# Value products of the merged stage: one 128-column stationary operand against two of 64 columns

## The chip, the cores and the metric

The kernel runs on one core of a Trainium2 chip. The metric is the device time of one execution in microseconds (us). TensorE (PE) multiplies, VectorE (DVE) and ScalarE (ACT) work element by element, GpSimd (POOL) does masks, powers and indirect transfers, SyncE (SP) issues most DMAs.

## The reference, cut to what matters

A block of 8 sequences of 512 tokens, width 1024, fp32. First an mLSTM attention with 16 heads of 64, gated and added to x; then a layernorm and a mixture of 16 experts (two per token) with a shared feed-forward network, gated and added.

```
C  = qk * D                               # per head: 512 x 512, lower triangle, decayed
Cn = C / (normalizer + EPS)
h  = einsum('bhst,bhtd->bhsd', Cn, vh)    # the value products
x  = x + tanh(g_xattn) * (layernorm of h per head, times ln_scale)
x  = x + tanh(g_ffn) * (shared(xn) + routed(xn))      # xn = layernorm(x)
```

## The kernel before, in words

The program is two blocks, one after the other.

**The merged stage** (`mix_block`) handles the 4096 tokens in 32 chunks of 128. The chunk has number c = 4b + j: b is the sequence, j its chunk of four. Attention runs chunk by chunk: within a chunk the products of 128 queries with 128 keys, and a `state` (per head 64 x 65) that carries what came before in the sequence, so for j = 0 there is no state to read and for j = 3 none to write. The same stage computes layernorm, router and the first half of the shared feed-forward network (`gate_up`, L1009, and `stage_y`, L1022) for earlier chunks. `ORDER` is a list written out by hand: each of 35 turns goes through the items of `TURN`, each for its own chunk (offset), and every engine does its part of each item in that order. So every engine runs its own fixed queue, and semaphores are the only coupling.

In a turn TensorE comes, in this order, to these items. A2 is the gate products (L978). B0 and B1 are the scores (L1033), H1 a transpose (L946), A3 the gate rows (L984). **B2** is the value products of heads 0 to 7, and with j > 0 their state products (L1051). Then come Y1 to Y4 (L1022), with B1 and A5 between them; A5 transposes the gate rows (L991) and waits for the semaphore `rows_rdy`, which VectorE raises with L723. N1 transposes the first half of xn into `p_tr` (L946). **B3** is the value products of heads 8 to 15. A6 is a tiny product for the decay (L996). N2 transposes the second half of xn into the same `p_tr`, so it waits until ScalarE (L555) and VectorE (L863) have read the first half. After that come G1 to G6 (L1009), B4 (L1078: the new state, j < 3), E3 (L1090, router, waits for L863 on the second half), Q2, Q3, and K7, K8 (L1009).

The value products of a group of four heads are the loop at L1044 and L1045. The stationary operand is `cmat` of a head (128 keys in the partitions, 128 query tokens as columns), the moving operand `ctx_v` (128 keys, 64 values and a column of ones, so 65 columns). The result, 128 tokens x 65, goes into the bank `p_u[g % 2]`. `start` is set for the first head of a group, `stop` only where no state product follows. All operands are fp32, and in the trace each such product is two MATMUL records and two LDWEIGHTS records: 8 heads are "x16".

The state products of B4 (L1078) have the same moving operand, and 64 stationary columns (`ks`, one head); the even heads write partitions 0 to 63 of the bank, the odd ones 64 to 127.

VectorE makes `cmat` (L752, two groups for B2, two for B3), which raises `c_rdy`. ScalarE copies the results out (L595) when `u_ps` is raised.

**The VectorE chain that ends at L723.** After gate-up of the turn is done: ScalarE's tanh (L617), VectorE L869, L872, then L800 (needs the power of GpSimd, L469, which needs L792), L694, L752 twice, L878, L698, L699, L808 (needs GpSimd L477, which stands behind L469 and two indirect DMAs, L490), L810 to L814, L704 to L723. L792 comes earlier in the turn, behind L737, which needs ScalarE's L547, which needs the transfer of the row `mid_s_row` (SP, L364).

**The expert stage** (`ffn_block`) is 105 tiles of 128 rows; the change doesn't touch it.

Of the kernel before, what the change touches and what calls it, by code (L numbers as in the profile page):

```python
# [11 lines left out]
P = 128  # L12
# [7 lines left out]
HV = DH + 1  # L20
# [14 lines left out]
def ge(eng, sem, n):  # L35

    if isinstance(n, int) and n <= 0:
        return
    eng.wait_ge(sem, n)
# [32 lines left out]
def mix_block(nc, t, keep):  # L72
# [3 lines left out]
    with ExitStack() as ctx:  # L76
        def sb(name, shape, dt=f32):
            return ctx.enter_context(nc.sbuf_tensor(name, shape, dt))

        def pb(name, shape, dt=f32):  # L80
            return ctx.enter_context(nc.psum_tensor(name, shape, dt))
# [27 lines left out]
        cmat = stage[:, 8, :].rearrange("p (n g s) -> p n g s", n=2, g=HG)  # L109
        x = stage[:, 10, :]  # L110
        sq = stage[:, 11, :].rearrange("p (h d) -> p h d", h=NH)
        ctx_v = sb("ctx_v", [P, 2, NH, HV])
# [14 lines left out]
        rows = sb("rows", [NH, 4, P])  # L127
# [17 lines left out]
        p_u = [pb(f"p_u{n}", [P, 512]) for n in range(2)]  # L145
# [92 lines left out]
        def heads(g):  # L238

            return [8 * (g // 2) + g % 2 + 2 * n for n in range(HG)]  # L240
# [694 lines left out]
        def _(pe):  # L935
# [101 lines left out]
            def values(b, j, gs):  # L1037
                c = b * CPB + j
                for g in gs:
                    pe.wait_ge(c_rdy, NG * c + g + 1)  # L1040
                    ge(pe, u_rdy, NG * c + g - 1)
                    if g < 2:
                        ge(pe, state_rdy, 2 * states_done(b, j))
                    for n, h in enumerate(heads(g)):  # L1044
                        last = nc.tensor.matmul(p_u[g % 2][:, n * HV:(n + 1) * HV], cmat[:, g % 2, n, :], ctx_v[:, j % 2, h, :],  # L1045
                                                start=(n == 0), stop=(j == 0), skip_group_check=True)
                if j > 0:
                    for n, pair in enumerate(zip(heads(gs[0]), heads(gs[1]))):
                        for h in pair:
                            lo = DH * (h % 2)  # L1050
                            last = nc.tensor.matmul(p_u[h % 2][:, n * HV:(n + 1) * HV], qs_t[lo:lo + DH, j % 2, h // 2, :],  # L1051
                                                    state[lo:lo + DH, h // 2, :], start=False, stop=True,
                                                    skip_group_check=True)
                last.then_inc(u_ps, 2)

            def states_done(b, j):
                return (CPB - 1) * b + j

            def stage_b(part, b, j):
                c = b * CPB + j  # L1060
                if part < 2:
                    scores(b, j, (2 * part, 2 * part + 1))
                if part == 2:
                    if j > 0:
                        pe.wait_ge(qs_sb, scaled_before(b, j) + 1)
                    pe.wait_ge(cv_in[j % 2], 16 * (2 * b + j // 2) + 16)
                    values(b, j, (0, 1))
                if part == 3:
                    values(b, j, (2, 3))
                if part == 4:  # L1070
                    if j < CPB - 1:
                        pe.wait_ge(ks_rdy, states_done(b, j) + 1)
                        for m in range(2):
                            pe.wait_ge(u_rdy, NG * c + 3 + m)
                            for n in range(8):
                                h = 8 * m + n
                                lo = DH * (h % 2)
                                last = nc.tensor.matmul(p_u[m][lo:lo + DH, (n // 2) * HV:(n // 2 + 1) * HV],  # L1078
                                                        ks[:, h, :], ctx_v[:, j % 2, h, :], start=True, stop=True)
                            last.then_inc(ds_ps, 1)  # L1080
# [557 lines left out]
```

## Time and profile before

| | |
|---|---|
| time, median of 3 runs | 3005.92 us (3003.09 to 3010.25) |
| the profiled execution's own time | 2988.08 us |
| its span | 2986.5 us |
| TensorE busy | 2848.8 us (95%) |
| VectorE busy | 1869.6 us (63%) |
| mean granted TensorE clock | 0.986 of full speed |

The span is that of the profiled execution; 1.6 us of its time lie outside. The merged stage takes roughly the first 1120 us, the experts the rest. A busy TensorE is a row of matmul records whose ends are modelled and overlap, so that its pace is to be read from starts.

### The profile page before, as it was taken

The numbers are of one execution on the slowest core, as the hardware profiler recorded it, in microseconds if no ns is written. First come the engines' busy times: TensorE is split into PE (matmuls) and PEld (weight loads), VectorE is DVE, ScalarE is ACT, GpSimd is POOL, SyncE is SP. The second block draws the span as 40 slices with busy tenths as digits, with TensorE's granted clock in tenths as the row PEclk, the third lists the DMA queues.
The fourth block names the chain that finished last, engine by engine and source line by source line (L and its number), as shares of the span: only waits on it lengthen the run. The fifth ranks groups of instructions, "written<-read, shape, count | busy, mean of one in ns | idle before, by whom it ended". The sixth has DMA issues, their size and how long they took to land.

```text
span 2986.5 us, 47577 instructions
## 1 busy us (share of the span) xinstructions
PE 2848.8 (95%) x16422; PEld 2354.5 (79%) x16423; DVE 1869.6 (63%) x3213; ACT 1008.7 (34%) x1916; POOL 978.6 (33%) x1089
## 2 busy tenths in 40 slices
PE   4799999999999997999999999999999999999999
PEld 3688888888888875788888888888888888888887
DVE  3788888888888865454554545545545446565665
ACT  4444444444444421233333333333333331111111
POOL 1333333334333423443343343433434411111111
PEclk9799999999999998999999999999999999999999
DMA  6445445554555442344444344443444325444544
GB/s 194 143 152 173 143 150 152 165 157 151 150 164 154 149 149 81 138 148 148 142 148 145 141 155 141 147 148 142 148 146 144 116 98 162 158 158 149 167 141 161
DMA packets 229289, 441.87 MB, mean 148 GB/s; under 512 B 98832, under 2 KB 115088, under 8 KB 228624
## 3 DMA queue, kind: packets, MB, share of 16 engines
q1 hardware_dynamic: 123504, 333.62, 32.6%
q0 software_dynamic: 35008, 73.10, 7.8%
q10 hardware_dynamic: 70656, 33.56, 4.4%
q8 instruction: 73, 1.20, 0.2%
q14 instruction: 48, 0.39, 0.0%
HBM read 350.83 MB, written 107.18 MB: 153 GB/s over the span
## 4 chain that ended last, share of the span: by engine, by line
PE 57%; DVE 1%; ACT 1%; issue 0%; ACTq 0%; DMA 0%; POOL 0%; POOLq 0%; DVEq 0%
PE p_g_b L1561 19%; PE p_up_b L1561 19%; PE p_y_b L1549 18%; PE p_h_b L1536 2%; DVE w_lo L1411 1%; ACT w_hi L1353 1%; ACTq L1194 0%; DMA xn<-mid_xn,idx_q 0%; DVE x_t_b L1437 0%; ACTq L1179 0%; DMA idx<-mid_lists 0%; POOL idx L1289 0%; POOL xn L1299 0%; DVE x L1477 0%; DVE x L1468 0%
## 5 line engine op out<-in xcount | busy, mean ns | idle before, releaser
L1299 POOL DMA_INDIRECT xn<-mid_xn,idx_q x288 | 306.0, 1063 | 565.0 <-DVE x_t_b L1437 474.7
L1561 PE MATMUL p_g_b<-w_hi,xt_hi_b 128*128 128x512 f32 x840 | 339.6, 404 | 29.5 <-DVE w_lo L1411 13.4
L1427 DVE TENSOR_TENSOR ht_lo_b<-p_h_b,ht_hi_b 128x512 fp32r<-128x512 f32 x105 | 72.3, 689 | 470.8 <-ACT ht_hi_b L1365 470.8
L1549 PE MATMUL p_y_b<-w_hi,ht_hi_b 128*128 128x512 f32 x840 | 327.1, 389 | 1.9 <-DVE ht_lo_b L1427 1.9
L1561 PE MATMUL p_up_b<-w_hi,xt_lo_b 128*128 128x512 f32 x840 | 328.6, 391 | 0.0
L1561 PE MATMUL p_g_b<-w_hi,xt_lo_b 128*128 128x512 f32 x840 | 328.5, 391 | 0.0
L1561 PE MATMUL p_up_b<-w_hi,xt_hi_b 128*128 128x512 f32 x840 | 328.5, 391 | 0.0
L1561 PE MATMUL p_up_b<-w_lo,xt_hi_b 128*128 128x512 f32 x840 | 328.4, 391 | 0.0
L1561 PE MATMUL p_g_b<-w_lo,xt_hi_b 128*128 128x512 f32 x840 | 327.9, 390 | 0.0
L1549 PE MATMUL p_y_b<-w_hi,ht_lo_b 128*128 128x512 f32 x840 | 326.9, 389 | 0.0
L1549 PE MATMUL p_y_b<-w_lo,ht_hi_b 128*128 128x512 f32 x840 | 326.9, 389 | 0.0
L1411 DVE TENSOR_TENSOR w_lo<-stage,w_hi 128x1024 fp32r<-128x1024 f32 x200 | 230.0, 1217 | 80.0 <-ACT w_hi L1360 52.6
L1437 DVE STREAM_TRANSPOSE x_t_b<-xn 128x1024 f32<-128x1024 f32 x105 | 237.0, 2257 | 21.5 <-DMA xn<-mid_xn,idx_q 10.2
L1365 ACT ACTIVATE ht_hi_b<-p_h_b 128x512 fp32r<-128x512 f32 x105 | 62.9, 599 | 546.5 <-PE p_h_b L1536 546.5
L1396 ACT ACTIVATE th_b<-p_g_b 128x512 f32<-128x512 f32 x105 | 62.8, 598 | 520.5 <-PE p_up_b L1561 520.5
L1449 DVE SCALAR_TENSOR_TENSOR th_b<-th_b,p_g_b 128x512 f32<-128x512 f32 x105 | 72.1, 687 | 254.7 <-ACT th_b L1396 254.7
L1009 PE MATMUL p_g<-w_hi,xt 128*128 128x512 f32 x512 | 212.4, 415 | 0.0
L1561 PEld LDWEIGHTS p_g_b<-w_hi,xt_hi_b 128*128 128x128 f32 x840 | 158.5, 189 | 65.5 <-DVE w_lo L1411 19.0
L1009 PE MATMUL p_up<-w_hi,xt 128*128 128x512 f32 x512 | 201.7, 394 | 0.0
L1549 PEld LDWEIGHTS p_y_b<-w_hi,ht_hi_b 128*128 128x128 f32 x840 | 157.7, 188 | 34.9 <-DVE ht_lo_b L1427 2.2
L1561 PEld LDWEIGHTS p_up_b<-w_lo,xt_hi_b 128*128 128x128 f32 x840 | 158.2, 188 | 33.9
L1561 PEld LDWEIGHTS p_g_b<-w_hi,xt_lo_b 128*128 128x128 f32 x840 | 158.2, 188 | 33.9
(223 smaller groups left out, 5797.0 us busy)
## 6 DMA issues: line engine op xcount, KB each, us to landing
mid_y<-y_b SPq DMA_DIRECT2D x73, 512.0 KB, 2.6
stage<-mid_g_row SPq DMA_DIRECT2D x64, 512.0 KB, 5.6
stage<-in_eg SPq DMA_DIRECT2D x16, 2048.0 KB, 8.9
stage<-in_eu SPq DMA_DIRECT2D x16, 2048.0 KB, 15.2
stage<-in_ed SPq DMA_DIRECT2D x16, 2048.0 KB, 19.4
mid_y<-in_x SPq DMA_DIRECT2D x34, 512.0 KB
stage<-in_x SPq DMA_DIRECT2D x32, 512.0 KB
stage<-in_ctx_t ACTq DMA_DIRECT2D x32, 512.0 KB, 8.5
```

What stands on the lines that cost most here:

```text
L1009: last = nc.tensor.matmul(out[:, :], xt[:, a, k, :], w[:, k, o:o + FE], start=(k == 0 and m == 0), stop=(k == KD - 1 and m == 2))
L1299: nc.gpsimd.indirect_dma_start(out=xg_parts[:, n, :], out_offset=None, in_=xn_flat, in_offset=bass.IndirectOffsetOnAxis(ap=idx_q[:, n:n + ...
L1353: nc.scalar.activation(w_hi[:, p, :], stage[:, p, :], ACT.Copy).then_inc(gu_hi, 1)
L1365: nc.scalar.activation(ht_hi[:, :, :], p_h[:, :, :], ACT.Copy).then_inc(ht_hi_rdy, 1)
L1396: nc.scalar.activation(th[:, :], p_g[:, :], ACT.Tanh, scale=0.5).then_inc(tanh_rdy, 1)
L1411: nc.vector.tensor_tensor(w_lo[:, p, :], stage[:, p, :], w_hi[:, p, :].bitcast(f32), ALU.subtract).then_inc(sem_lo, 1)
L1427: nc.vector.tensor_tensor(ht_lo[:, :, :], p_h[:, :, :], ht_hi[:, :, :].bitcast(f32), ALU.subtract).then_inc(ht_rdy, 1)
L1437: nc.vector.transpose(x_t[:, :, :].rearrange("p k (j t) -> p t k j", t=4), xg_parts[:, :, :].rearrange("p t (i k) -> p t k i", k=KD)).then ...
L1449: nc.vector.scalar_tensor_tensor(out=th[:, :], in0=th[:, :], scalar=1.0, in1=p_g[:, :], op0=ALU.add, op1=ALU.mult).then_inc(silu_step, 1)
L1536: last = nc.tensor.transpose(p_h[:, k, :], h[:, k * P:(k + 1) * P], ident[:, :])
L1549: last = nc.tensor.matmul(p_y[n][:, :], a[:, k, :], b[:, GUP + k, w], start=(k == 0 and m == 0), stop=(k == FE // P - 1 and m == 2))
L1561: mm = nc.tensor.matmul(out[:, :], a[:, k, :], w[:, k, o:o + FE], start=(k == 0 and m == 0), stop=(k == KD - 1 and m == 2))
```

## The change

Each value product is written as two. The first takes columns 0 to 63 of `cmat` of the head (tokens 0 to 63) and writes partitions 0 to 63 of `p_u`, the second takes columns 64 to 127 and writes partitions 64 to 127. Both have the same moving operand. `start` and `stop` are as before, for either half. The number of products at this line goes from 512 to 1024.

```diff
                     for n, h in enumerate(heads(g)):
-                        last = nc.tensor.matmul(p_u[g % 2][:, n * HV:(n + 1) * HV], cmat[:, g % 2, n, :], ctx_v[:, j % 2, h, :],
-                                                start=(n == 0), stop=(j == 0), skip_group_check=True)
+                        for o in (0, P // 2):
+                            rows = slice(o, o + P // 2)
+                            last = nc.tensor.matmul(p_u[g % 2][rows, n * HV:(n + 1) * HV], cmat[:, g % 2, n, rows],
+                                                    ctx_v[:, j % 2, h, :], start=(n == 0), stop=(j == 0),
+                                                    skip_group_check=True)
```

## Rows read from the trace of the kernel before

**Rows 1.** The page: busy time of each engine, share of the span, instructions
```profile
PE 2848.8 (95%) x16422; PEld 2354.5 (79%) x16423; DVE 1869.6 (63%) x3213; ACT 1008.7 (34%) x1916; POOL 978.6 (33%) x1089
```

**Rows 2.** Stretches: length, busy PE, PEld, DVE, ACT, POOL, granted clock, DMA share, GB/s
```profile
75.00:150.00 75.00, 58.83 (x487) 50.81 (x486) 56.21 (x123) 35.40 (x76) 24.09 (x15) 0.73 0.48 142
...
450.00:600.00 150.00, 145.24 (x1174) 120.91 (x1174) 127.46 (x307) 68.13 (x166) 56.02 (x39) 1.00 0.52 160
```

**Rows 3.** Waits, 150 to 1050 us: waiter <- releaser: total us, times, longest
```profile
PE p_small L978 <- issue: 22.0, 27, 0.8
PE p_small L991 <- DVE rows L723: 2.7, 7, 0.6
...
ACT stage L547 <- DMA stage<-mid_s_row: 9.7, 10, 1.8
```

**Rows 4.** TensorE by time (start us, us): B2 of a chunk with j > 0
```profile
510.12 2.00 PE L1045 MATMUL p_u<-ctx_v,stage 128*128 128x65 f32 x16
512.04 1.11 PE L1051 MATMUL p_u<-state,stage 64*128 64x65 f32 x16
```

**Rows 5.** The same turn: N1, B3 and the state products behind it
```profile
520.44 0.60 PE L946 MATMUL p_tr<-ident,xn 128*128 128x128 f32 x4
520.87 1.90 PE L1045 MATMUL p_u<-ctx_v,stage 128*128 128x65 f32 x16
522.70 1.11 PE L1051 MATMUL p_u<-state,stage 64*128 64x65 f32 x16
```

**Rows 6.** The same turn: end of G1, B4 and start of E3
```profile
525.16 0.39 PE L1009 MATMUL p_g<-w_lo,xt 128*128 128x512 f32 x1
525.39 0.40 PE L1009 MATMUL p_up<-w_lo,xt 128*128 128x512 f32 x1
525.72 1.15 PE L1078 MATMUL p_u<-ctx_v,stage 128*64 128x65 f32 x32
526.80 1.96 PE L1090 MATMUL p_small<-rw,xt 128*128 128x32 f32 x16
```

**Rows 7.** Instructions on p_u: ns min/median/max, first and last start, form
```profile
L1045 PEld LDWEIGHTS p_u<-ctx_v,stage x1024: 186/192/338, 40.8 to 1091.0; 128*128 128x128 f32 x171
...
L1078 PEld LDWEIGHTS p_u<-ctx_v,stage x768: 132/138/232, 54.0 to 1059.7; 128*64 128x64 f32 x192
```

**Rows 8.** Two turns with j = 0: B2, and L723 with A5 behind it
```profile
309.74 2.00 PE L1045 MATMUL p_u<-ctx_v,stage 128*128 128x65 f32 x16
311.55 0.71 PE L1022 MATMUL p_g<-w_hi,ht 128*128 128x512 f32 x2
...
316.34 0.27 DVE L723 SCALAR_TENSOR_TENSOR rows<-fcum,gmax 16x128 f32<-16x128 f32 x1
...
317.17 0.35 PE L991 MATMUL p_small<-ident,rows 16*128 16x16 f32 x3
...
450.41 0.27 DVE L723 SCALAR_TENSOR_TENSOR rows<-fcum,gmax 16x128 f32<-16x128 f32 x1
...
450.83 0.33 PE L991 MATMUL p_small<-ident,rows 16*128 16x16 f32 x3 [0.37 <-DVE rows L723]
```

**Rows 9.** L723 and A5 in the turn of rows 4
```profile
517.32 0.27 DVE L723 SCALAR_TENSOR_TENSOR rows<-fcum,gmax 16x128 f32<-16x128 f32 x1
...
518.72 0.29 PE L991 MATMUL p_small<-ident,rows 16*128 16x16 f32 x2
```

**Rows 10.** A turn with j = 0: L863 on the first half, then N2
```profile
320.36 0.69 DVE L863 TENSOR_TENSOR xt<-p_tr,xt 128x512 fp32r<-128x512 f32 x1 [0.47 <-ACT xt L555]
...
321.54 0.66 PE L946 MATMUL p_tr<-ident,xn 128*128 128x128 f32 x4
```

**Rows 11.** ScalarE and VectorE later in the turn of rows 4
```profile
531.80 1.06 ACT L547 ACTIVATE stage<-stage 128x1024 f32<-128x1024 f32 x1 [0.38 <-DMA stage<-mid_s_row]
...
534.58 1.22 DVE L737 SCALAR_TENSOR_TENSOR stage<-stage 128x1024 f32<-128x1024 f32 x1
...
540.07 0.69 DVE L869 SCALAR_TENSOR_TENSOR th<-th,p_g 128x512 f32<-128x512 f32 x1 [1.63 <-ACT th L617]
```

## The prediction

> **What bounds the kernel now.** I read the page first for the busiest engine, then the stretches of the merged stage, then the waits, then TensorE in order of time around the changed line. On the page TensorE is busy 95% of the span, the next engine 63% [rows 1]. In the middle of the merged stage TensorE is busy 145.2 of 150 us at the full clock, but VectorE is close behind it with 127.5 [rows 2]. The list of waits tells how much TensorE stands still from 150 to 1050 us: 22.0 us ahead of L978, 0.8 in each of 27 turns, and 2.7 us at A5, where it waits for VectorE's L723 in 7 of the 27 [rows 3]. The rest is its own queue, back to back. So a microsecond taken from TensorE's queue is one off the stage, as long as VectorE, GpSimd and the transfers have results ready that much sooner. Before 150 us it is otherwise: TensorE is busy 58.8 of 75 us and has 0.73 of its clock [rows 2].
>
> **What a value block costs now.** Busy times overlap, so I go by starts. B2 takes 512.04 - 510.12 = 1.92 us with state products behind it [rows 4], and 311.55 - 309.74 = 1.81 with none [rows 8]. B3 takes 522.70 - 520.87 = 1.83 [rows 5]. For 16 passes (8 heads, two each) that is 0.114 to 0.120 us a pass. There are 64 such blocks (1024 passes) [rows 7].
>
> **What it will cost.** The new form, 128 rows by 64 stationary columns, 65 moving ones, fp32, halves of a bank in turn, is in the trace already: it is B4. Its 32 passes take 526.80 - 525.72 = 1.08 us, 0.034 a pass [rows 6], less than a third of a full-width one. Two things can explain it, and the change gets both: the weight load is shorter (138 against 192 ns) [rows 7], and two passes on different halves of the columns run side by side. A changed block is 8 heads x 2 halves x 2 passes = 32 passes, so 1.08 us. Two differences from B4 remain. Both halves stream the same moving operand, where in B4 they are two heads; I cost that at nothing, since neither half can need more than its own read. And the state products behind it are a third form (64 rows by 128 columns).
>
> For that exit: L1045 ahead of the state products took 0.11 us more than ahead of Y1 (1.92 against 1.81). L1078 ahead of L1090 is a change of form too, so some of it is in the 1.08. Bounds 1.08 and 1.20; I take 1.14. For the entry: L1078 starts 0.33 us after the L1009 before it, where two L1009 are 0.23 apart [rows 6], so entering the narrow form costs 0.10. B3 comes from full-width transposes and pays it anew; B2 comes from the 16-column products of A3 and changes form today, so I put nothing there (bounds 0 and 0.10).
>
> The Trainium skill (TensorEngine Tiling (Array Packing), Key Properties) says that changing the tiling mode drains TensorE. This trace agrees, with 0.10 us for one change. By the rule alone, with 0.10 at every entry and exit, a block would save 0.1 less than I reckon, some 6 us over 64 blocks.
>
> So B2 saves 1.92 - 1.14 = 0.78 us (0.62 to 0.84), B3 saves 1.83 - 1.14 - 0.10 = 0.59 (0.53 to 0.75).
>
> **What of it reaches the end of the turn.** TensorE arrives earlier at everything behind B2 and B3, and three results may not be there.
>
> A5 waits for L723. In the turn of rows 4, L723 ends at 517.59 and A5 starts at 518.72, 1.13 later [rows 9]. In a turn that waits the gap is 450.83 - 450.68 = 0.15 [rows 8], so that is its least and the slack here 0.98: B2's 0.78 goes through. The 7 turns that wait already [rows 3] give nothing. With j = 0 there are no state products between, and in the turn of rows 8 that doesn't wait the gap is 317.17 - 316.61 = 0.56, so 0.4 goes through. Taking A5 of each turn in the same way, of the 28 turns from 140 us to 1050 us 21 have j > 0, and 4 of them no slack, the other 17 at least 0.65; of the 7 with j = 0, 3 have none and 4 have 0.4. B2 then brings 17 x 0.78 + 4 x 0.4 = 14.9 us.
>
> N2 waits for L863, which runs from N1, ahead of B3, and not from B3. With j = 0, L863 ends at 321.05 and N2 starts at 321.54 [rows 10]; with a least gap like that of A5 some 0.34 goes through. With j > 0 the state products, 1.11 us [rows 5], stand there as well, and the whole 0.59 does. B3 brings 21 x 0.59 + 7 x 0.34 = 14.8 us.
>
> The third is a transfer. The scaled queries are reloaded by a DMA whose start hangs on L723, not on B2 or B3. ScalarE's L547 behind it ends at 532.86, and VectorE takes it up at 534.58 [rows 11]: 1.72 us of slack, and the turn gets up to 1.37 shorter. That holds, barely. But ScalarE waited for this transfer 10 times, up to 1.8 us [rows 3], and there VectorE will wait. VectorE has 1.63 us of idleness ahead of L869 [rows 11] that hides this from TensorE at the end of the turn; not hidden is L792, from which GpSimd's power, its list writes, L808 and so L723 of the next turn follow. I take 0.3 us for each of 10 such turns, 3 us (bounds 0 and 10 x 1.37).
>
> The four turns outside, the first three and the last, have 8 blocks. In the first ones TensorE waits for VectorE, and what it does sooner only makes it wait longer; the last is like the others. I take 2 us for all (bounds 0 and 8).
>
> Within B2 the second group of heads will be asked for sooner, half a new block after the start (about 0.55 us where it was 0.96). L752 makes it just ahead; I cost this at nothing, at most 0.1 a turn, 3 us. Nothing on SP or POOL is added or moved, and ScalarE copies the same tiles.
>
> **Sum.** 14.9 + 14.8 + 2 - 3 = 28.7, say 29 us. The profiled execution took 2988.1, so 2959. The median of the runs shown is 3005.9, 18 us above that execution, and what separates them isn't in the trace; the saving is the same, and I forecast 3005.9 - 29 = 2977 us. All low ends together (B2 17 x 0.62 + 1.6, B3 21 x 0.53 + 2.4, less 14 and 3) leave 9 us, all high ones (17 x 0.84 + 1.6, 21 x 0.75 + 2.4, and 8) 42.
>
> **Rivals.**
>
> *All of it arrives.* A slack that grows along with the change (VectorE too gets its inputs sooner) would let every block through: 64 x (0.78 + 0.59) / 2 = 44 us, 2962. Against it: the chain to L723 starts ahead of B2. 12%.
>
> *VectorE and the transfer take over.* VectorE is at 127.5 of 150 us [rows 2]; in turns 1.4 us shorter it is at 89%, in order and with waits inside. If the late reload delays L792 in most turns, A5 waits in all of them, B2's gain is gone and B3's is halved in the turns with j = 0 and one in three of the others: about 10 us, 2996. For it are the 7 waits at A5 and the 10 of L547; against it that A5's median slack is 0.98. 22%.
>
> *The halves don't run side by side.* This is the slow side. The new passes share rows and moving operand, only the columns differ. Two passes of B4 take 2 x 0.034 = 0.0675 us; if they alternate two heads' data and that is what lets them overlap, 32 passes in a row cost 32 x 0.0675 = 2.16 us, with the exit 2.22. A block gets 0.3 (B2) to 0.49 (B3, with entry) slower, 64 x 0.4 = 25 us, 3031. It decides from 1.83 / 32 = 0.057 us a pass on. Against it is that B4 has the same rows for both halves too, and 0.034. 5%.
>
> Beside it: the Trainium skill (TensorE: Matmul & The Clock Gate, Part 3, The mechanism) says that a weight load overlaps a running matmul only when the row group differs. The passes of one block all have all rows, so by that rule they would stand in line. In B4 they do too, and 0.034 us a pass is less than half of either of its instructions' times, so this trace speaks against the rule for halves of the columns.
>
> *No difference* through something not seen, within 6 us: 7%, and slower for other causes (the granted clock falls below 1.00 in the middle of the stage): 1%.
>
> **How the numbers follow.** The forecast's own case has 53%; since its ends are not likely to meet, it spans some 18 to 38 us, 2968 to 2988. A measurement of this kernel can tell 0.2%, 6 us, from no change. Faster takes the forecast, the first rival and most of the second: 87%. Same 7%, slower 6%. For 8 in 10 the range reaches from 2960, just past where all of it arrives, to 2994, most of the way to the second rival.
>
> **What would show each step.** In the changed profile L1045's successor (the same loop) has x32 in a block, and starts 1.1 to 1.2 us apart from what follows, at full clock; 1.8 or more and the side-by-side step is wrong. The wait of L991 for L723 grows from 2.7 us and 7 times to some 10 us and 15 to 20 times; if it is in nearly all turns with over 0.5 us each, the second rival is right. N2 begins to wait in the turns with j = 0 only. VectorE's L737 waits for L547 in about 10 turns, and its wait at L869 shrinks. From 1200 us on nothing changes but the start. If the turn, 33.3 us on average now (27 of them in 900 us) [rows 3], is not 0.8 to 1.3 shorter, the prediction is wrong.

## The result, and the profile after

| | before | after |
|---|---|---|
| median of the runs | 3006.78 us (4 runs, 3003.09 to 3010.25) | 2981.11 us (4 runs, 2978.03 to 2983.26) |
| the profiled execution's own time | 2988.08 us | 2982.64 us |
| its span | 2986.5 us | 2981.0 us |

The ratio is 0.9914, with a 95% interval of 0.9901 to 0.9926: 26 us faster (22 to 30), where I forecast 29 and 2977 us. The two profiled executions are only 5.4 us apart. The one of before is 19 us under its median, the one of after 1.5 us over its own, so the two traces can't simply be subtracted.

The page after, busy time of each engine, and the stretch in the middle of the merged stage (columns as in [rows 2]):
```profile
PE 2798.5 (94%) x17446; PEld 2296.2 (77%) x17447; DVE 1876.4 (63%) x3213; ACT 1009.0 (34%) x1916; POOL 981.1 (33%) x1089
```
```profile
450.00:600.00 150.00, 139.41 (x1320) 114.07 (x1319) 130.35 (x301) 68.98 (x166) 56.77 (x39) 1.00 0.53 159
```
TensorE has 50.3 us less busy time than in [rows 1], and in the middle of the stage 139.4 us of 150 instead of 145.2 [rows 2]. It now stands still in places where it did not before.

TensorE in order of time, B2 and B3 of a turn with j > 0. The changed loop is now L1047; what stands behind it in the program has moved by three lines (L1051 is L1054, L1078 is L1081, L1090 is L1093):
```profile
508.55 1.15 PE L1047 MATMUL p_u<-ctx_v,stage 128*64 128x65 f32 x32
509.63 1.11 PE L1054 MATMUL p_u<-state,stage 64*128 64x65 f32 x16
...
517.76 0.26 PE L991 MATMUL p_small<-ident,rows 16*128 16x16 f32 x2 [1.37 <-DVE rows L723]
...
519.45 0.60 PE L946 MATMUL p_tr<-ident,xn 128*128 128x128 f32 x4
519.98 1.15 PE L1047 MATMUL p_u<-ctx_v,stage 128*64 128x65 f32 x32
521.06 1.11 PE L1054 MATMUL p_u<-state,stage 64*128 64x65 f32 x16
```
Both blocks take 1.08 us from start to start, where they took 1.92 and 1.83 [rows 4, 5]. Ahead of A5 (L991) TensorE stands still for 1.37 us, which eats all that B2 saves in this turn.

From the list of waits, 150 to 1050 us (total us, times, longest):
```profile
PE p_small L991 <- DVE rows L723: 17.2, 15, 2.5
...
DVE gparts L694 <- remote: 15.2, 12, 1.5
...
PE p_small L984 <- DVE gparts L694: 11.9, 14, 1.1
...
DVE stage L737 <- ACT stage L547: 5.7, 5, 2.4
...
PE p_u L1047 <- issue: 4.4, 6, 1.4
PE p_small L996 <- DVE decm L730: 3.6, 6, 0.6
```
The wait at A5 has grown from 2.7 to 17.2 us [rows 3], more than the some 10 us expected. Three others of TensorE are new: L984 waits for VectorE's L694, L1047 has idle time ahead of it, and L996 (A6) waits for L730.

**What stands behind L984.** Another turn of the changed kernel, the engines by time:
```profile
236.12 1.08 PE L978 MATMUL p_small<-stage,w_gate 128*32 128x128 f32 x32 [0.81 <-issue]
...
236.50 1.06 POOL L490 DMA_INDIRECT mid_lists<-tok,posi  x1 [0.19 <-issue]
...
238.23 0.66 PE L946 MATMUL p_tr<-ident,th 128*128 128x128 f32 x4
...
239.59 0.35 DVE L694 TENSOR_SCALAR gparts<-p_small,gate_bias 128x128 f32<-128x128 f32 x1 [1.51 <-remote]
239.81 0.60 ACT L623 ACTIVATE ht<-p_tr 128x512 fp32r<-128x512 f32 x1 [3.78 <-PE p_tr L946]
...
240.00 0.61 PE L984 MATMUL p_small<-gparts,fold 128*16 128x128 f32 x4 [1.11 <-DVE gparts L694]
```
and a turn of the kernel before:
```profile
406.01 1.06 POOL L490 DMA_INDIRECT mid_lists<-tok,posi  x1 [0.18 <-issue]
...
406.73 1.08 PE L978 MATMUL p_small<-stage,w_gate 128*32 128x128 f32 x32 [0.81 <-issue]
...
408.61 0.34 DVE L694 TENSOR_SCALAR gparts<-p_small,gate_bias 128x128 f32<-128x128 f32 x1
...
409.42 0.61 PE L984 MATMUL p_small<-gparts,fold 128*16 128x128 f32 x4
409.53 0.60 ACT L623 ACTIVATE ht<-p_tr 128x512 fp32r<-128x512 f32 x1 [2.90 <-PE p_tr L946]
```
L694 reads the result of L978, whose matmuls end at 237.20. In the turn of before L694 starts 1.88 us after L978's start, here 3.47 after, and VectorE is idle meanwhile. ScalarE's L623 needs only the transposes that start at 238.23, and waits as well.

The trace also keeps the time of every semaphore signal. In the turn above L978's comes 2.64 us behind the start of its last matmul, and L694 starts 0.02 us behind the signal. So the signal itself is late, and VectorE takes it up at once. Below I call these late signals. From 130 us on there are 28 turns. In the first trace of before L978's signal comes 0.31 us behind that start in all of them, here over 0.8 us behind in 18, at most 2.66. What comes in the first 1.07 us costs nothing, since VectorE isn't free for L694 before.

Where they occur they go with the place of the list writes (GpSimd's two indirect DMAs, L490) in the turn. In this trace all 22 turns in which the first write starts between 1.03 us ahead of L978's last matmul and 0.17 us behind it have a signal 0.6 us or more behind; the 6 turns in which it starts 0.4 us or more behind that matmul have none, 0.31 us as in the kernel before. But the first trace of before has writes in those same places, and no late signal.

### The profile page after: what moved, and what is told of

Same layout as the page of the kernel before. It is cut to its first block, busy times and chain, and to the rows that moved or that the text cites. A ratio compares the mean times of both kernels' runs of the same rounds, so it can differ in the third digit from the quotient of the medians.

```text
span 2981.0 us, 49625 instructions
## 1 busy us (share of the span) xinstructions
PE 2798.5 (94%) x17446; PEld 2296.2 (77%) x17447; DVE 1876.4 (63%) x3213; ACT 1009.0 (34%) x1916; POOL 981.1 (33%) x1089
## 4 chain that ended last, share of the span: by engine, by line
PE 57%; DVE 1%; ACT 1%; issue 1%; ACTq 0%; DMA 0%; POOL 0%; POOLq 0%; DVEq 0%
PE p_g_b L1564 19%; PE p_up_b L1564 19%; PE p_y_b L1552 17%; PE p_h_b L1539 2%; DVE w_lo L1414 1%; ACT w_hi L1356 1%; ACTq L1197 0%; DMA xn<-mid_xn,idx_q 0%; ACT xt_hi_b L1374 0%; DVE x_t_b L1440 0%; ACTq L1182 0%; DMA idx<-mid_lists 0%; POOL idx L1292 0%; POOL xn L1302 0%; DVE x L1480 0%
## 5 line engine op out<-in xcount | busy, mean ns | idle before, releaser
L584 ACT ACTIVATE stage<-stage,cols 128x128 f32<-128x128 f32 x512 | 154.2, 388 | 96.4 <-POOL stage L454 96.4
```

Source lines behind the costliest of these rows:

```text
L584: nc.scalar.activation(gbd[:, h, :], gbd[:, h, :], ACT.Exp, bias=cols[:, j, 0, h:h + 1]).then_inc(d_rdy, 1)
```

## The experiments

Each was compared with runs of the kernel before on the same chip. The first four shared one chip (kernel before: 3005.3 us), the next four a second (3001.6), the last four a third (2990.4). The kernel before and the changed kernel, unedited, have traces on the first chip only (the chip of the result's two isn't on record).

**1 and 2: the two kernels again.** No edit.

> The kernel before, unchanged, for a second trace of it. The profiled execution of before took 2988 us, its four timed ones 3003 to 3010, and the changed kernel's trace shows something that before's doesn't: the semaphores that TensorE raises at L978, L1033 and L946 (A2, B0, H1) reach VectorE and ScalarE up to 2.7 us after the last matmul where 0.3 is usual. Theory D (density): the narrow passes cause it, so this trace has none of it, at any span. Theory E (execution): it comes and goes with the execution, costs the kernel before the 18 us that part 2988 from 3006, and this trace has a span near 3004 with waits of VectorE's L694 or L752 of about 15 to 20 us in the merged stage. Time against before: ratio 1.000 within 0.002 by both.

> The changed kernel, unchanged, on the same chip as the kernels beside it. By the working of the prediction 26 to 29 us less than before, ratio 0.990 to 0.992. Theory D: the late semaphores at A2 to H1 are there again in about 15 of 28 turns. Theory E: their number differs from the first trace, and the time goes with it.

Before: 3006.67 us (ratio 1.0004, 0.9993 to 1.0014); after: 2979.32 us (0.9914, 0.9899 to 0.9929). Waits of before, 150 to 1050 us, in an execution nearer to its median (3000.96 us):
```profile
DVE gparts L694 <- remote: 4.4, 4, 1.4
PE p_small L991 <- DVE rows L723: 4.2, 11, 0.6
PE p_small L984 <- DVE gparts L694: 3.3, 5, 1.0
PE p_u L1045 <- issue: 2.6, 2, 1.3
```
The kernel before has late signals too, and the trace I predicted from just had none. By their own times there are as many as in the changed kernel (18 of 28 turns over 0.8 us, 19 in the changed kernel's second trace). They cost it less: past the point where VectorE is free for L694 they reach 7.7 us in all, in the changed kernel's two traces 17.3 and 15.1 (150 to 1050 us). The waits of L694 and L752 that theory E put at 15 to 20 us are 6.9.

This execution also shows the granted clock at 0.5 (1.2 GHz) for 6.8 us (length, busy PE, PEld, DVE, ACT, POOL, granted clock, DMA share, GB/s):
```profile
742.00:750.00 8.00, 5.89 (x74) 4.65 (x72) 5.90 (x17) 1.71 (x3) 7.27 (x4) 1.00 0.44 157
750.00:756.80 6.80, 6.80 (x35) 5.53 (x33) 6.41 (x18) 2.57 (x5) 0.62 (x2) 0.51 0.20 46
```
TensorE had been busy 5.89 of the 8 us ahead of it. In the first trace of before the clock is 1.00 from 150 to 1050 us throughout. In the changed kernel's second trace L984 waits for L694 12 times, 8.9 us, and L991 for L723 13 times, 14.7 us.

**3 and 4: one half of the change alone.** `B2 only`: heads 0 to 7 split, heads 8 to 15 as before. `B3 only`: the other way.
```diff
-                        for o in (0, P // 2):
-                            rows = slice(o, o + P // 2)
+                        for o, m in (((0, P // 2), (P // 2, P // 2)) if g < 2 else ((0, P),)):
+                            rows = slice(o, o + m)
```

> Only B2 (groups 0 and 1) is split, B3 stays at full width. Theory 1 (the working of the prediction): each B2 0.78 us shorter, A5 absorbs some, 15 us less than before, ratio 0.995. Rival (VectorE's chain to L723 is the bound at A5 in most turns): B2's gain is gone there, 0 to 4 us, ratio 0.999 to 1.000, and TensorE's wait at L991 grows by about what B2 saved.

> Only B3 (groups 2 and 3) is split. Theory 1: 0.59 us in each turn with j > 0, 0.34 with j = 0: 15 us less than before, ratio 0.995, and the sum of this run's and the last one's gains is that of the whole change. Rival (VectorE and the reload bound the turn): the first of the two splits brings most and the second little, so that each alone gives 20 us or more.

B2 only: 2994.15 us, ratio 0.9966 (0.9953 to 0.9978), 10 us. B3 only: 2999.58 us, 0.9980 (0.9968 to 0.9992), 6 us. Both expectations are missed: each part was to give 15 us, and the parts give 16 together, the whole 26. Waits of B2 only, then of B3 only:
```profile
PE p_small L991 <- DVE rows L723: 23.7, 16, 2.5
...
PE p_small L984 <- DVE gparts L694: 4.7, 9, 0.7
```
```profile
PE p_small L984 <- DVE gparts L694: 11.1, 14, 1.0
...
PE p_u L1047 <- issue: 7.0, 11, 1.2
...
PE p_small L996 <- DVE decm L730: 4.1, 7, 0.6
```
Most of what B2 alone doesn't bring is lost at A5, and much of B3's at L984, L1047 and A6. The trace of B3 only is that of its slowest execution, 9 us over its median, with the granted clock at 0.5 for 20.4 us between 150 and 1050 us, so its waits are at the high end. Why the whole loses less at A5 (14.7 to 17.2 us) than B2 alone (23.7) isn't settled.

**5 and 6: no list writes.** Here a small power on GpSimd takes the place of each of the two list writes, in both kernels (1.35 us each, the writes 1.20). It leaves out what the writes do: the lists stay zero, so the experts gather other rows, as many as before.
```diff
-                        nc.gpsimd.indirect_dma_start(
...
+                        nc.gpsimd.tensor_tensor(idle[:, k, :], idle[:, k, :], mhalf[:, 0:5], ALU.pow).then_inc(done, 1)
```

> The kernel before, where GpSimd doesn't write the token lists: each of its two indirect DMAs a turn (L490) is an arithmetic instruction of about the same length, so that its queue keeps its timing. What is left out: the lists stay zero and the experts get token 0's rows; tiles and their number stay. Theory S (the late signals come with GpSimd's indirect DMAs beside A2, B0 and H1): no late signal at A2 in this trace, and the merged stage ends some 10 to 18 us sooner, as in the first trace of before. Theory N (they have nothing to do with them): late signals at A2 in over half the turns, as in the second trace of before, and the merged stage ends within 4 us of that.

> The same omission in the changed kernel. Theory S: no late signals, and the change is worth here what the prediction's working gives without them, 29 us less than the run beside it (within 5). Theory N: late signals in 20 of 28 turns as before, and the difference to the run beside it is the 26 us of the full kernels.

Before: 2978.76 us (0.9915, 0.9901 to 0.9929); after: 2945.43 us (0.9805, 0.9790 to 0.9819). Without list writes the change is worth 33.3 us, and no signal of L978 is late. Waits of TensorE from 150 to 1050 us without list writes, in the kernel before (these are all), then the larger ones in the changed kernel:
```profile
PE p_small L978 <- issue: 22.0, 27, 0.8
PE p_small L1090 <- DVE xt L863: 1.5, 7, 0.5
```
```profile
PE p_small L978 <- issue: 19.5, 24, 0.8
PE p_small L991 <- DVE rows L723: 6.8, 7, 1.4
PE p_small L996 <- DVE decm L730: 4.2, 7, 0.6
...
```
The kernel before gains 22.8 us by it, but not all of that is late signals: the undisturbed execution, with list writes and none late, took 2988. Up to the last L978 the two traces take the same time (1039.3 and 1040.0 us); the 5 us by which the trace without list writes is shorter lie behind it, where the experts gather other rows. In the changed kernel without list writes A5 starts at its least gap behind L723, 0.15 to 0.17 us, in 21 of 28 turns: here VectorE's chain is what TensorE runs up against next.

**7 and 8: list writes at the end of the turn** (an item of their own behind D1; on GpSimd they then run behind L477).

```diff
...
-                "E4", "W6", "Z1", "U1", "D1", "K7", "K8", "Q3")
+                "E4", "W6", "Z1", "U1", "D1", "M1", "K7", "K8", "Q3")
...
```

> The kernel before, all of its work, with GpSimd's two list writes of a turn moved behind L477 of the same turn, so that they start about 4.5 us after A2 instead of 0. GpSimd's L477 comes 0.8 us sooner at best. Theory S: the late signals leave A2, B0 and H1 and could turn up 4 us later, beside B2 and B1; time 5 to 15 us less than before. Theory N: late signals at A2 as ever; time within 3 us of before, or up to 5 less for the earlier L477.

> The changed kernel with the same move. Here A5 waits for L723, and L723 for L477, in half of the turns, so that the earlier L477 counts. Theory S: 10 to 20 us less than the changed kernel, 2960 to 2970. Theory N: 3 to 8 us less, 2972 to 2977.

Before: 2999.55 us (0.9996, 0.9985 to 1.0007); after: 2980.02 us (0.9916, 0.9901 to 0.9931). No signal of L978 is late in either, and the time has not moved. No theory holds whole: in the first S had 5 to 15 us less and N late signals as ever, in the second both had 2977 us or less. Other waits are there instead. Changed kernel with the writes moved (its lines behind L487 stand three further on: L697 is L694, L539 is L536, L981 is L978, L987 is L984):
```profile
POOL stage L454 <- DMA stage<-mid_g_row: 138.8, 51, 6.3
...
PE p_small L987 <- DVE gparts L697: 13.1, 19, 1.0
...
PE p_small L981 <- ACT stage L539: 12.2, 15, 0.8
```
GpSimd waits 138.8 us for the reload of the gating row, in the changed kernel 47.5. L987 waits for L697 as long as it did with late signals, so that wait alone doesn't tell of them.

The four kernels of this chip have no late signal at all, and none of them has the list writes in their old place. So experiments 5 to 8 by themselves don't tell whether the writes or the chip make the difference; for the writes speaks their place in the turns of the traces above.

**9: halves apart.** Loops over heads and halves exchanged; the same 32 passes, but eight in a row on the same columns.
```diff
-                    for n, h in enumerate(heads(g)):
-                        for o in (0, P // 2):
+                    for o in (0, P // 2):
+                        for n, h in enumerate(heads(g)):
```

> The changed kernel with the loops over heads and over halves exchanged: first all passes on columns 0 to 63 of four heads, then all on columns 64 to 127. The same 32 passes in a block, the same shapes, but 8 passes in a row (4 heads, two each) go to the same half of TensorE, and halves change once in a group of four heads. Theory A (the halves run side by side, and that is what makes a pass 0.034 us; alone, a pass of this shape takes over half of a full-width one, some 0.058 us): the block takes 32 x 0.058 = 1.9 us against 1.09 in the changed kernel, and the time is within -5 to +15 us of the kernel before. Rival B (the pass is short because its weight load is of 64 columns and not 128, in whatever order): a block takes 1.05 to 1.15 us and the time stays at the changed kernel's 2980 us, within 4. Between 1.2 and 1.7 us a block both have a share, and the block's start-to-start says how much of the 0.8 us each has.

2974.76 us on the third chip, where the kernel before takes 2990.43 (0.9949, 0.9935 to 0.9964): 15.7 us less. TensorE, by time:
```profile
237.45 1.55 PE L1047 MATMUL p_u<-ctx_v,stage 128*64 128x65 f32 x32
238.93 1.11 PE L1054 MATMUL p_u<-state,stage 64*128 64x65 f32 x16
```
A block takes 1.48 us, 0.046 a pass: between the theories. Of the 0.84 us that B2 saves, 1.92 - 1.48 = 0.44 comes with the half width even when the same columns are used again and again, and 1.48 - 1.08 = 0.40 from alternating between the halves. No signal was late in this execution, with the list writes in their old place.

**10 to 12: list writes in the middle of the turn**, in a stretch where GpSimd is idle, some 9 to 11 us behind A2: in the kernel before, in the changed kernel, and in the changed one with A5 an item later (the edit shown).
```diff
-        TURN = (... "Y1", "E1", "P1", "A4", ... "Y3", "A5", "J1", "Y4", "N1", ...
+        TURN = (... "Y1", "E1", "M1", "P1", "A4", ... "Y3", "J1", "Y4", "A5", "N1", ...
```

> The kernel before with GpSimd's two indirect list writes of a turn as an item of their own behind E1, so that they run some 9 us behind A2 instead of beside it, in a stretch where GpSimd is idle. Theory S (the semaphores that TensorE raises at the gate products come up to 2.7 us late only while a list write runs on GpSimd beside them, and this is what TensorE loses when VectorE's L694 waits for them): no wait of VectorE at L694 behind TensorE over 0.5 us in the profile, and since the power that L808 needs no longer stands behind the writes, no new wait for it; the time is 0 to 15 us under the kernel before (it had 0 to 27 such turns in its profiled executions). Rival R (something else in the turn makes them late, the writes in any place, or the power): L694 waits as often, or the lateness moves to other TensorE semaphores (B1, Y1 or B2), and the time is within 5 us of the kernel before.

> The changed kernel with the list writes moved in the same way. Theory S: the late signals at A2 are gone here too, and the place is free of the waits that the earlier move brought (ScalarE and VectorE behind one another at L539, the transfer of the gating row), so the split is worth what it was with no list writes at all: 28 to 33 us over the moved kernel before, some 2955 to 2970 us. Rival R: L984 waits for L694 as often as in the changed kernel (8 to 12 us in all), the split is worth 20 to 26 us over the moved kernel before, and the time is 2975 to 2985.

> The kernel of the run ahead of this with A5 (the transpose of the gate rows, which waits for VectorE's L723) moved one item back, behind Y4, so that TensorE reaches it about 0.7 us later. If A5's wait is what B2's share of the gain was lost on (14.7 to 17.2 us in the changed kernel's profiles, 6.8 with no list writes): that wait falls to under 3 us in all and the time is 3 to 10 us under the run ahead. Rival: what hangs on A5 (the gate rows' sums, A6, VectorE's chain to the state) comes later by the same amount and TensorE waits at L996 or L1093 instead; within 3 us of the run ahead, or slower.

All three are slower than the kernel before on that chip: 3012.95 us (1.0079, 1.0066 to 1.0092), 3004.99 (1.0050, 1.0037 to 1.0063) and 3006.80 (1.0049, 1.0036 to 1.0062). No expectation had that. No signal was late in any of them, but none was in experiment 9 either, on the same chip with the writes in their old place. DMAs by tile in the kernel before, 150 to 1050 us (KB each, median us from issue to landing), then in the changed one with the writes in the middle:
```profile
mid_g_row<-neg_g SPq DMA_DIRECT2D x27, 8.0 KB, 1.4
```
```profile
mid_g_row<-neg_g SPq DMA_DIRECT2D x26, 8.0 KB, 4.4
```
The gating row (8 KB) is written out and read back on SP (L348, L354). With the list writes just ahead of it, the write takes 4.4 us instead of 1.4 (1.4 in the changed kernel as well, 3.6 and 3.7 in experiments 7 and 8). In the kernel with the writes in the middle and no split, SP and GpSimd in one turn:
```profile
494.58 1.07 POOL L493 DMA_INDIRECT mid_lists<-tok,posi  x1 [0.22 <-issue]
495.95 1.17 POOL L493 DMA_INDIRECT mid_lists<-tok,posi  x1 [0.30 <-issue]
...
497.75 0.36 SPq L348 DMA_DIRECT2D mid_g_row<-neg_g  x1
...
501.87 0.81 SPq L354 DMA_DIRECT2D stage<-mid_g_row  x2
...
506.89 1.09 POOL L454 TENSOR_SCALAR_AFFINE_SELECT stage<-stage 128x1024 f32<-128x1024 f32 x1 [2.69 <-DMA stage<-mid_g_row]
```
4.12 us pass between L348 and L354, and L454, ScalarE's work behind it and VectorE's L740 (L737) follow late. In the last kernel A5's wait is gone and A6's has grown from 4.3 to 15.0 us (14 times). But the kernel of experiment 11 waits at A5 only 2.8 us, 7 times, so there was little left to gain there, and what moving A5 does in the changed kernel proper stays untested. The split is worth 8.0 us between the first two (3012.95 and 3004.99).

The clock may have a part in the loss. Between 150 and 1050 us it is at 0.5 for 17.0, 34.0 and 37.4 us in the three traces (10.2 and 17.0 in experiments 7 and 8), against 3.4 in either trace of the changed kernel and none in the first of before (on this chip the kernel before has no trace). One such stretch of experiment 11 (columns as above):
```profile
882.80:889.60 6.80, 5.19 (x53) 4.25 (x54) 5.61 (x17) 1.72 (x4) 3.66 (x2) 0.50 0.62 224
```
At half the clock TensorE does at least half of its full pace, so by my estimate at most half of these times is lost, 8 to 19 us.

## Why the prediction was right, point by point

**The block, its exit and entry: right.** I took 1.14 us for B2 and 1.24 for B3 with its entry; measured are 1.08 start to start for both. Ahead of the state products the exit is at the low bound. With j = 0, ahead of Y1, B2 takes 1.17 (median of 7 turns) instead of 1.81. The entry is there: from the first transpose to B3's start it is 519.98 - 519.45 = 0.53 us, before it was 0.43 [rows 5], the 0.10 expected. So with j > 0 B2 saves 0.84 and B3 0.75 - 0.10 = 0.65. The Trainium skill's rule that a change of tiling mode drains TensorE (TensorEngine Tiling (Array Packing), Key Properties) fits that 0.10.

**Halves side by side: right, and the slow rival could not have come.** Its price was 2.16 us a block, from 0.0675 us a pass without overlap of the halves. Experiment 9 has hardly any alternation, and a pass takes 0.046, under the 0.057 from which the rival decides. I had named two explanations for B4's 0.034, and the half width and the alternation have about half of the saving each. The Trainium skill (TensorE: Matmul & The Clock Gate, Part 3, The mechanism) lets weight loads overlap matmuls only with other row groups. Here all passes have all rows, and start 0.034 us apart with weight loads of 138 ns each (L1047, median); its rule doesn't hold for these, as the records show them.

**B2's share lost at A5: right in kind, too small.** I expected some 10 us in 15 to 20 turns; it is 17.2 in 15, and 14.7 in 13 in the second trace. With no signal late it is 11.5 in 13 (experiment 9, where B2 saves less) and 6.8 in 7 without list writes.

**N2 waits in turns with j = 0: wrong in place and in size.** N2 (L946) waits nowhere. A6 stands between B3 and N2 and waits for VectorE's L730, which stands in VectorE's queue behind L863 on the first half, and L863 runs from N1. I had listed A6 in the order and not asked what it needs. The turn of [rows 10], before and after:
```profile
320.96 0.21 DVE L730 TENSOR_SCALAR decm<-headmask,dec 16x8 f32<-16x8 f32 x1
...
321.23 0.38 PE L996 MATMUL p_small<-decm,headsel 16*128 16x8 f32 x2
```
```profile
316.80 0.69 DVE L863 TENSOR_TENSOR xt<-p_tr,xt 128x512 fp32r<-128x512 f32 x1
...
317.40 0.21 DVE L730 TENSOR_SCALAR decm<-headmask,dec 16x8 f32<-16x8 f32 x1
...
317.67 0.38 PE L996 MATMUL p_small<-decm,headsel 16*128 16x8 f32 x2 [0.61 <-DVE decm L730]
```
A6 starts 0.06 us behind the end of L730 in both: it had no slack before the change either, though TensorE showed no idle time ahead of it. From N1's first matmul to A6 it is 2.29 us, in all 7 such turns of before and in 6 of the 7 after. So in those turns nothing of B3's 0.65 gets past A6, where I let 0.34 of 0.59 through: the term 7 x 0.34 = 2.4 us was nothing.

**The reload: within its bounds, fewer and longer.** VectorE waits at L737 5.7 us in 5 turns (2.6 in 3 in the second trace) where I expected about 10 turns and 3 us. What of it reaches TensorE no run shows. Its idle time ahead of L869 shrank from 36.8 to 21.5 us, as expected.

**The turn 0.8 to 1.3 us shorter: not met.** This was my own sign of being wrong. From A2 to A2 the turns of chunks 8 to 28 take 33.37 us in the first trace of before and 33.86 in the second, 33.48 and 33.25 after. The second traces are 0.61 apart, the first 0.11 the other way. Only without list writes is the turn shorter by what I asked: 33.24 and 32.32, 0.92. The undisturbed working (29 us) belongs to that case, where 33.3 was measured, and is 4 too low there. With list writes the changed kernel loses 8.9 to 11.9 us at L984 and 4.4 to 5.1 at L1047, that the kernel before loses only in part (3.3 and 2.6 in its second trace). The 26 us measured would be the higher saving less that, and less what A5 loses beyond it; these parts were not measured one by one. That 29 came so close owes something to luck: the working was 4 us too low for a kernel without late signals, and it had no term for them.

**The term that I left open** was the 18 us between the profiled execution and the median, "the saving is the same". It isn't quite: late signals and a fall of the clock are what the second trace of before has more of, 13 us later by its own time, and the changed kernel has more of the first. Of the rivals, 44 us and 10 us are both outside the interval. That VectorE takes over is true in part: its chain to L723 sets A5 in half of the turns.

**What stays open.** What makes a signal late. Five traces have late signals (both of the changed kernel, the second of before, B2 only, B3 only), with 140 turns from 130 us on. In the 115 in which the first list write starts between 1.5 us ahead of L978's last matmul and 0.22 us behind it, the signal comes 0.58 us or more behind that matmul's start, in the other 25 it comes after 0.31. So the writes have a part in it. But the first trace of before and that of experiment 9 have the writes in the same places and no late signal, so the writes alone don't do it. On the third chip the kernel before has a median of 2990.4 us, near the undisturbed 2988. That would fit a chip on which it doesn't occur; the changed kernel was not run there, nor was the kernel before profiled. And every move of the writes brought waits and falls of the clock of its own, so what the late signals alone cost was not measured. No version tried beats the changed kernel with its work whole; halves apart is on record on the third chip only.

## What to carry to other kernels

Where a stationary operand is 128 columns wide, the moving one short (65 columns) and all is fp32, splitting it into halves of 64 and alternating between them cut TensorE's time for a block from 1.92 to 1.08 us; half of that needs the alternation, so put the loop over halves innermost (what the order is worth in the whole kernel was not measured on one chip). Where several chains arrive within a microsecond of their use, price the saving turn by turn at every wait behind it, small items like A6 too. An engine without idle time ahead of an item can still have no slack there: compare the item's start with the end of what it needs. And look at a second profiled execution before trusting the slack. The same split was worth 33 us with two small DMAs a turn left out, 26 with them in place, and 20 and 8 with them moved. Small indirect writes moved to 2 to 7 us ahead of a small write that something waits for made it land after 3.6 to 4.4 us instead of 1.4, and brought the whole kernel nothing in five tries.

## What the runs showed of the hardware that I had not expected

- TensorE's signals can come late while GpSimd issues an indirect DMA: L978's up to 2.66 us behind the start of its last matmul instead of 0.31, in turns where the first DMA starts up to 1.5 us ahead of that matmul or at most 0.22 us behind it; L694 then starts 3.47 instead of 1.88 us behind L978's start. Other executions have the DMA in the same place and no late signal.
- A write of 8 KB by SP lands after 4.4 us (median, experiment 11) instead of 1.4 with two indirect DMAs of GpSimd ahead of it.
- 128 x 64 fp32 passes start 0.046 us apart on the same columns, 0.034 on alternating ones, 0.114 to 0.120 at full width: twice the passes take 0.77 of the time even with hardly any alternation.
- The granted clock can fall to 1.2 GHz for 6.8 us in the middle of a stage where TensorE is busy nearly throughout (750 to 757 us in the second trace of before). Such falls add up to 34.0 us between 150 and 1050 us in experiment 11, and to none in the first trace of before.
